# Four attentions and four feed-forward layers on one core: every sublayer turns to the first half of its tokens first

## What is computed

```python
# sublayer 0 and, but for the weights, 4 (causal softmax attention)
att = jnp.einsum('bhqd,bhkd->bhqk', q, k) / math.sqrt(HEAD_DIM)
att = jnp.where(causal, -1e9, att)
out = jnp.einsum('bhqk,bhkd->bhqd', softmax(att), v)          # then @ w_out.T
# sublayer 2: 16 query heads, 4 key heads, rope, window of 64, two softmaxes
p1 = softmax(q1 @ k1.T * scale + neg);  p2 = softmax(q2 @ k2.T * scale + neg)
# (p1 - lam * p2), negative values cut to 0, rows normalised, @ v, @ Wo
# sublayer 6: scores * tril before the softmax, so tokens behind the query count with exp(0)
# x = layernorm(x + sublayer(x)), eight times
```

## Time and profile before

| | |
|---|---|
| median of 3 runs | 1172.81 us (1171.85 to 1173.26) |
| the profiled execution's own time | 1171.49 us |
| its span, first to last instruction | 1169.7 us |
| busy | PE 1005.7 us (86%), DVE 698.5 (60%), ACT 541.8 (46%), POOL 332.7 (28%) |
| mean granted TensorE clock | 0.907 of full speed |
| sublayers 0 to 7, from last normalisation to last normalisation | 210.4, 61.8, 187.4, 176.9, 223.4, 22.9, 221.9, 65.0 us (the last to the end of the span) |

### The profile page before, as it was taken

How to read it: one execution, slowest core, us unless ns; L and a number is a source line. 1 busy time by engine, 2 the same in 40 slices (tenths; PEclk the granted TensorE clock), 3 DMA queues, 4 the chain that set the end, 5 groups by cost and what they waited for, 6 DMA issues and landing times. The chain is left out here.

```text
span 1169.7 us, 16510 instructions
## 1 busy us (share of the span) xinstructions
PE 1005.7 (86%) x5954; PEld 573.3 (49%) x5954; DVE 698.5 (60%) x1986; ACT 541.8 (46%) x1145; POOL 332.7 (28%) x464
## 2 busy tenths in 40 slices
PE   6999998787998868899998899887777988888785
PEld 2545454673444535337356444444454544445575
DVE  2667773775376873532322358778282677876665
ACT  3566655333579862110112456664314455556422
POOL 3202122331367870000002111112461144532222
PEclk9989998998789977899998969999778889999898
...
GB/s 229 1 1 1 1 1 1 50 1 159 1 1 2 2 1 92 14 1 1 0 1 1 0 1 109 1 1 1 1 1 1 0 1 1 2 1 1 1 18 19
DMA packets 4165, 21.12 MB, mean 18 GB/s; under 512 B 345, under 2 KB 1625, under 8 KB 3060
## 3 DMA queue, kind: packets, MB, share of 16 engines
...
## 5 line engine op out<-in xcount | busy, mean ns | idle before, releaser
L890 ACT ACTIVATE PB<-pair 128x1024 f32<-128x1024 f32 (+3 forms) x288 | 223.1, 811 | 140.8 <-PE pair L1609 139.6
L1126 DVE CUSTOM_DVE_ANT_0 junk<-bank,cst 128x128 bf16<-128x128 f32 (+3 forms) x384 | 171.5, 487 | 127.8 <-PE bank L1593 125.7
L724 POOL TENSOR_SCALAR_AFFINE_SELECT PB<-PB 128x256 f32<-128x256 f32 x192 | 79.0, 415 | 330.4 <-ACT PB L890 328.7
L1129 DVE TENSOR_REDUCE pmx<-bank 128x1 f32<-128x512 f32 x192 | 122.8, 684 | 49.7 <-PE bank L1593 48.9
L1593 PE MATMUL bank<-KO_r,QO_r 64*128 64x512 f32 (+3 forms) x576 | 138.4, 417 | 11.7 <-DVE A L1204 3.9
L1625 PE MATMUL pvb<-PB,V 128*32 128x512 f32 (+3 forms) x1152 | 128.2, 517 | 11.8 <-ACT PB L890 8.2
L1605 PE MATMUL pair<-QO_r,KO_r 64*128 64x512 f32 (+3 forms) x576 | 115.7, 393 | 15.8 <-ACT PB L890 14.8
L1593 PEld LDWEIGHTS bank<-KO_r,QO_r 64*128 64x128 f32 x576 | 71.6, 191 | 111.7 <-DVE pmx L1126 40.2
L730 POOL TENSOR_TENSOR parts_r<-y_f,parts_r 128x512 fp32r<-128x512 f32 x24 | 30.6, 1276 | 321.2 <-ACT parts_r L861 321.2
L1609 PE MATMUL pair<-ms,sel_r 64*128 64x512 f32 (+3 forms) x576 | 102.5, 349 | 0.0
L948 ACT ACTIVATE KO<-pair,nm 128x128 f32<-128x128 f32 x256 | 91.6, 434 | 22.1 <-DVE nm L1268 22.0
...
## 6 DMA issues: line engine op xcount, KB each, us to landing
...
```

The lines of the kernel that those rows point to most:

```text
L724: pool.affine_select(p2, p2, pattern=[[0, 2], [1, P]], compare_op=ALU.is_ge, fill=0.0, base=0, channel_multiplier=-1).then_inc(causal, 1)
L890: act.activation(pb[:, st % 2, 2 * i:2 * i + 2, 0:n], ps[:, :, 0:n], ACT.Exp, scale=scale)\
L1126: r_done(dve.tensor_tensor_reduce(junk[:, (r_used - 1) % 3, 0:n], ps[:, 0:n], tri[:, HALF - n:HALF], 1.0, LOWEST, ALU.add, ALU.max, accum_ ...
L1129: r_done(dve.tensor_reduce(to, ps[:, 0:n], AX.X, ALU.max))
```

## The change

`OUT_FIRST` becomes 0 everywhere, so every sublayer delivers tokens 0 to 511 first. `STAGES` takes the first half of all four head groups, then the second half of all four. `operands` gives all operands of one half before `x1` and those of the other behind it. In sublayer 2 all six `R`, twelve `s` and `v` stand before the loop; the loop keeps eight `s`, one behind every second unit. The shifted V isn't projected any more: two DMAs copy it from `v_own`. The normalisation of the first half is cut in three and spread over three units. `em` has four buffers for two.

```diff
+W_E = ND + 12 + 2 * ND
-OUT_FIRST = {ATT: 1, GLU: 1, WATT: 1, MOE: 1, BIN: 1, TERN: 1}
+OUT_FIRST = {ATT: 0, GLU: 0, WATT: 0, MOE: 0, BIN: 0, TERN: 0}
-STAGES = [(0, 0), (0, 1), (1, 1), (2, 1), (3, 1), (3, 0), (2, 0), (1, 0)]
+STAGES = [(0, 0), (1, 0), (2, 0), (3, 0), (0, 1), (1, 1), (2, 1), (3, 1)]
@@ operands
-    early = [build("b", side, 0, first) for side in "qk"] + [build("s", side, 0, first) for side in "qk"] \
-        + [build("s", "q", 1, first), ("x1",)] + [build("b", side, 0, second) for side in "qk"] \
...
+    for half in (first, second):
+        if half == second:
+            plan.append(("x1",))
+        for hi in range(2):
+            plan += [build("b", side, hi, half) for side in "qk"]
+            plan += [build("s", side, g, half) for g in (2 * hi, 2 * hi + 1) for side in "qk"]
+            if hi == 0:
+                plan += [("v", k) for k in (2 * half, 2 * half + 1)]
@@ attention_plan, ready
-            return max(clock.e[0], done[("x1",)])
+            return max(clock.e[0], done[("x1",)] if item[1] // 2 == second else 0)
@@ windowed_plan
-T_ORDER = [W_FIRST + k for k in (1, 2, 3, 0)] + [W_LAST + k for k in range(TH)]
+W_HALVES = [(2, W_SOON), (2, W_LATE)] + [(tile, half) for half in (W_OUT, W_END) for tile in range(2)]
+T_ORDER = [TH * half + k for half in (W_OUT, W_END) for k in range(TH)]
+    before = [("R", 0), ("x1",), ("R", 1), ("R", 2), ("R", 3)] + rows("k", (0,), W_SOON) + rows("k", (0,), W_LATE) \
+        + rows("q", (0, 1), W_OUT) + [("R", 4)] + rows("q", (2, 3), W_OUT) + [("R", 5), ("v",)]
+    late = rows("q", range(NG), W_END)
...
+            if k % 2 and late:
+                plan.append(late.pop(0))
...
+        if 0 <= step < 8:
+            plan.append([("outT",), ("proj", 0), ("proj", 1), ("proj", 2), ("proj", 3), ("norm", 0), ("norm", 1),
+                         ("norm", 2)][step])
@@ sync, behind the loads of sublayer 2
+                    sp.wait_ge(v_there, 1)
+                    sp.wait_ge(w_blank, 1)
+                    load(v_to[WIN:P, :], v_from[0:WIN, :], v_moved)
+                    load(v_to[0:WIN, row:], v_from[WIN:P, 0:(NT - 1) * row], v_moved)
@@ tensor, windowed, pv 0
-                            pe.wait_ge(r_free, v_at)
+                            pe.wait_ge(v_there, 1)
+                            pe.wait_ge(v_moved, 32)
```

More of the change, by code:

```diff
@@ L177, in build @@
         return kind, side, g, half
[L179 to L186 removed]
+    plan = []
+    for half in (first, second):
[6 more added lines that the diff above has]
+                plan += [("v", k) for k in (2 * half, 2 * half + 1)]
+    return plan
 LEAN = 600
@@ L384, in attention_plan, with rows @@
     return plan
-W_TILES = (2, 0, 1)
-W_HALVES = [(tile, half) for half in halves_in(SUBLAYERS.index(WATT)) for tile in W_TILES]
-W_LAST, W_FIRST = TH * halves_in(SUBLAYERS.index(WATT))[1], TH * halves_in(SUBLAYERS.index(WATT))[0]
-T_ORDER = [W_FIRST + k for k in (1, 2, 3, 0)] + [W_LAST + k for k in range(TH)]
+W_SOON, W_LATE = halves_in(SUBLAYERS.index(WATT))
+W_OUT, W_END = halves_out(SUBLAYERS.index(WATT))
+W_FIRST = TH * W_OUT
+W_HALVES = [(2, W_SOON), (2, W_LATE)] + [(tile, half) for half in (W_OUT, W_END) for tile in range(2)]
+T_ORDER = [TH * half + k for half in (W_OUT, W_END) for k in range(TH)]
 UNITS = [(t, g) for t in T_ORDER for g in range(NG)]
 def windowed_plan():
-    first, second = W_HALVES[0][1], W_HALVES[-1][1]
-    def rows(side, g, half):
-        return [("s", side, g, x, half) for x in range(TWO)]
-    before = [("R", 0), ("x1",), ("R", 1), ("R", 2)] + rows("k", 0, first) + rows("q", 0, first) + rows("q", 1, first)
-    after = {k: [] for k in range(len(UNITS))}
-    after[0] = rows("q", 2, first)
-    after[1] = rows("q", 3, first)
-    for i, k in ((3, 2), (4, 4), (5, 6)):
-        after[k].append(("R", i))
-    after[3].append(("v",))
-    for x in range(TWO):
-        after[6 + x].append(("s", "k", 0, x, second))
-        for g in range(NG):
-            after[8 + TWO * g + x].append(("s", "q", g, x, second))
+    def rows(side, groups, half):
+        return [("s", side, g, x, half) for g in groups for x in range(TWO)]
+    before = [("R", 0), ("x1",), ("R", 1), ("R", 2), ("R", 3)] + rows("k", (0,), W_SOON) + rows("k", (0,), W_LATE) \
+        + rows("q", (0, 1), W_OUT) + [("R", 4)] + rows("q", (2, 3), W_OUT) + [("R", 5), ("v",)]
+    late = rows("q", range(NG), W_END)
     plan = []
@@ L427, in windowed_plan @@
         step = j - NG * TH - 2
-        if 0 <= step < 6:
-            plan.append([("outT",), ("proj", 0), ("proj", 1), ("proj", 2), ("proj", 3), ("norm",)][step])
+        if 0 <= step < 8:
+            plan.append([("outT",), ("proj", 0), ("proj", 1), ("proj", 2), ("proj", 3), ("norm", 0), ("norm", 1),
+                         ("norm", 2)][step])
     last = NT - 1
@@ L472, in uses_of_r @@
     for item in W_BEFORE + W_PLAN:
-        n += {"R": 2, "v": 2, "uT": 1, "accT": 1, "outT": ND, "proj": 1}.get(item[0], 0)
+        n += {"R": 2, "v": 1, "uT": 1, "accT": 1, "outT": ND, "proj": 1}.get(item[0], 0)
         if item == ("uT", gi):
@@ L1060, in post, with normalise, refine @@
                 normalise(s, k)
[L1062 removed]
+            def normalise(s, k, which=(0, 1, 2)):
                 t0 = halves_out(s)[k] * TH
[L1064 to L1066 removed]
                 v, y, w = lnv[:, 0, :], lnv[:, 1, :], lnv[:, 2, :]
[L1068 to L1072 removed]
+                def refine():
                     step(dve.scalar_tensor_tensor(w, y, -0.5, y, ALU.mult, ALU.mult))
@@ L1259, in windowed @@
                             middle(i - 1)
-                middle(2)
-                turned = []
+                    if item[0] == "v":
+                        middle(len(W_HALVES) - 1)
+                        ps = r_slot()[:, :].rearrange("p (t h d) -> p t h d", t=NT, h=KV)
+                        last = dve.tensor_copy(v_own[:, :, :, 0:HD], ps)
+                        r_done(last)
+                        r_wait()
+                        dve.nop().then_inc(v_there, 1)
                 for item in W_PLAN:
@@ L1688, in windowed @@
                         last.then_inc(e_full, 1)
+                    if item[0] == "v":
+                        w = w_att(s, 2 * D + 2 * KV * HD, KV * HD)
+                        ps = r_slot()
+                        for t in range(NT):
+                            last = over_width(ps[:, t * KV * HD:(t + 1) * KV * HD], lambda c: xT[:, c, t * P:(t + 1) * P],
+                                              lambda c: w[:, c, :])
+                        last.then_inc(r_full, 1)
                 uT_at = {}
```

92 lines of the change are left out of this document (26 added, 66 removed).

## The result

The changed kernel takes 1188.57 us (median of four executions, 1184.82 to 1190.67). The kernel before took 1172.33 beside it; the ratio is 1.012, 95% interval 1.0084 to 1.0157. It is slower by about 16 us, where I had forecast 10.5 us less.

The account below looks back on a forecast made before the run. Attentions taken as bound by TensorE's stream, sublayer 2 by a chain of hand-overs. Heads -9.5, attention 0 and tails 0, sublayer 2 -1: -10.5 from 1172.8 gives 1162 us; range 1146 to 1180, the forecast's own 1154 to 1169.

Parts of the forecast that it names:

- Heads: Starts of attentions 4 and 6: filling TensorE's idle and part of its lower clock gives -9.5 us, bounds 0 and -25.
- the stretch behind the head: Attentions 4 and 6, after the head: clock of 0.77 stays, 0 taken; full clock would give 11 us each at most.
- Attention 0: Whole attention: first maxima at the end of the loads in both orders, same work behind: 0, bounds -3 and +3.
- Tails: Ends of attentions: lone stage 17.9 us, output work moves to the middle at about equal cost: 0 each, bounds -3 and +3.
- rival on VectorE: Middle of attentions: maxima queue behind normalisation and residuals if VectorE is over about 90% busy: 1179 us or more, chance 0.20.
- the wait of 8.2 us for the weights' sums: Attentions: moves from the short stages to the start of stage (2, 1)'s exponentials and keeps its 8.2 us.
- Sublayer 2: Windowed sublayer: prefix +28, units -27 and cut normalisation -2 make -1 us, bounds -11 and +11.
- prefix: Sublayer 2, start to first exponential: 50 us where it was 21.9, so +28, bounds +23 and +33.
- units 0 to 15: Sublayer 2's loop: sixteen units, now holding only eight `s`, take 54 us for 81.1: -27, bounds -22 and -30.
- cut normalisation: Sublayer 2, first half's normalisation in three pieces fills VectorE's holes: -2.0 us, bounds 0 and -4.5.
- prefix not paid back: Sublayer 2: prefix +33 and units -22 make +9 after the normalisation, 1172 us; chance 0.20 together with heads giving nothing.
- three signs of being wrong: VectorE over 90% busy where `norm` stands, sublayer 2's prefix over 55 us, clock behind the heads over 0.1 from 0.77.

Follow-up runs that it names:

- e13: Kernel before, with four useless TensorE matmuls in each `s` ahead of the first `max` of attentions 4 and 6: 1166.5 us, ratio 0.9947.
- e6: e3 with both `exp` of a block ahead of the previous block's `pv` where no `max` is left: 1163.8 us, ratio to before 0.9894.
- e3: Changed kernel, attentions' first-half output work (turning, projecting, normalising) held back until no maximum is left: 1172.7 us, ratio to before 0.9967.
- e5: Changed kernel, first half's normalisation in the three attentions doing twelve refinements for three: 1213.3 us in one execution.
- e12: Kernel before, with both `exp` of a block ahead of the previous block's `pv` where no `max` is left: ratio 1.0001.
- e11: Changed kernel, with two `s` of the keys' first half ahead of `R` 3 in sublayer 2: 1188.5 us in one execution.
- e4: Changed kernel, mask matmul of sublayer 2's units 0 to 15 done three times for once, as TensorE filler: 1188.9 us.
- e9: Changed kernel, first half's normalisation in sublayer 2 whole behind one unit again: 1192.6 us in one execution.

## Why the prediction was wrong

**Heads: right in kind, 24 us for 9.5.** Attention 0 has no head to win and lost 8.8; measured against it, attention 4 gained 5.9 + 8.8 = 14.7 and attention 6 0.9 + 8.8 = 9.7. This is a rough measure: it takes the rest of the three attentions to lose alike, and single executions of one attention differ by up to 5.5 us. The failed step is the one on the stretch behind the head, "I take 0 and keep -11 as a bound". e13 shows for attention 4 that the holes of the head cost that stretch its clock: with filler in them and the order unchanged, the head gave 1.0 us and the stretch behind it 3.8, 5.2 over the whole attention. The Trainium skill, "TensorE: Matmul & The Clock Gate", Part 1, says that the clock falls to half after idle and rises when TensorE has been kept busy. The trace agrees in direction: 0.76 over the 64.8 us, 0.89 by filler alone, 0.92 with the change. I had set it aside because TensorE is 95% busy in the stretch behind, and what keeps so busy a stretch at 0.77 is still not shown; but idle ahead of it was part of it. The rest of the gain of attention 4, 14.7 - 5.2 = 9.5 us, is the idle and the order itself. How it splits between these wasn't measured.

**Attention 0: 0 forecast, +8.8.** It pays for the middle and the lone stage and has no head in return, and with both mended it takes 210.5 us (e6).

**Tails: 0 forecast, and this was the largest error in the attentions.** "It stands in the middle now, where it costs about as much" failed. The middle stage took 35.0, 35.1 and 37.0 us, and without that work beside it (e3) 23.9, 23.9 and 24.0. That work is 6.5 us of TensorE's time in either place; the step left out that maxima queue behind it on VectorE, some 5 us more. So of attention 0's 8.8 us, 11.2 - 6.2 = 5.0 go by e3 to where that work stands, and the lone stage took 21.0 us for the 17.9 that I had priced, 3.1 more; 0.7 is left over. My rival on VectorE named the place and the mechanism, but not its condition: it said over 90% busy, and the stage ends by VectorE at 74% (e5). The share is a mean over parts: one in which TensorE is full and maxima fall behind, and one of 5.3 us in which VectorE makes them up, busy 98%. The lone stage, 17.9 us by columns, took 21.0 to 21.2: it goes by hand-overs, 2.85 us for a full block, and e6 brought it to 17.1. From last `m` to last `acc` it was 22.0 to 22.3 us, not 18 to 20. One step held: the wait of 8.2 us for the weights' sums moved and kept its length (8.2 in the changed kernel).

**Sublayer 2: -1 forecast, +16.8.** The 16.8 us are against the first profile, where the old order took 187.4; it took 193.9 in e12 and 185.9 in e13, so 10 to 18 us. Term by term:

| term | forecast | measured | what the runs showed |
|---|---|---|---|
| prefix | +28 (to 50) | +33.8 (to 55.7) | 2 to 3.5 of 5.7 from ScalarE's order (e11); `R` 4 took 6.31 for 4.94 |
| units 0 to 15 | -27 (to 54) | -17.3 (to 63.8) | clock 0.63; the three units with `pv` 19.0 for 12.0; 4.7 came back with filler (e4) |
| cut normalisation | -2 | 0 | VectorE busy 19.11 of 20.5 (e9) |
| units 16 to 25 | 0 | +1.9 | clock 0.90 for 0.95; the old order took 36.6 at 0.80 in e12 |
| the rest | 0 | -1.6 | 28.6 for 30.2; the old order took 28.4 in e12 |

The two failed steps are of one kind. For the prefix I had followed VectorE's chain and TensorE's, but not ScalarE's queue. For the units I priced them by rows at a clock of 0.94, and thinned out TensorE's work in the same breath: three `R` and `v` went away from beside them. With less to do TensorE was granted 0.63. That is dear where TensorE is what a unit waits for: units 7, 11 and 15, with `pv`, took 6.2, 6.4 and 6.4 us, 7.0 of the 9.8 over my 54. I had priced each at 4.0, from rows in which units 11 and 15 took 4.1 and 4.3 at full clock. Unit 7 of the same profile took 6.3 at 0.51, so the price at the lower clock stood there to be read. In e4 the three take 4.4, 4.4 and 4.2 at full clock; of the 5.1 us that still separate its 59.1 from 54, 4 are in the first four units, where the filler itself ran at the lower level in units 2 and 3 (clocks 0.50 and 0.58). The rival "prefix not paid back" had the right sign, with +9 where +16.8 came.

So the whole: 24.4 gained in the heads, 3 x 8.8 = 26.4 lost in middle and tail, 16.8 lost in sublayer 2: 18.8 slower. The first two are worked out from one another, so only their difference is measured. Of the three signs of being wrong that I named, VectorE over 90% didn't come (74%), the prefix over 55 us did (55.7), and so did the clock behind the heads (0.93 over the 51.3 us that had 0.77). The heads' gain, larger than forecast, hid nearly all of what the attentions lost.
